# ScalarE's order within a slot: a sum's copy ahead of the scan's exponentials, in a one-core decoder layer

## What is computed

```
x = x + mamba(layernorm(x))            # dA = exp(dt*A); h = dA*h + dt*B*x; y = sum_n h*C; + D*x; 16 states
x = x + cross_attention(layernorm(x), ctx, mask)   # rmsnorm, 32 heads of 128, keys and values from ctx
x = x + ffn(layernorm(x))              # x @ W.T + b plus 16 low-rank experts
```

## Time and profile before

| | |
|---|---|
| median of three runs | 987.28 us (984.28 to 987.94) |
| the profiled execution | 985.46 us, span 983.5 us, granted TensorE clock 0.977 |
| TensorE busy | 938.3 us, 95% of the span |
| VectorE busy | 621.3 us, 63% |
| ScalarE busy | 517.1 us, 53% |
| GpSimd busy | 504.4 us, 51% |
| stage with sums and scan | to about 432 us |

### The profile page before, as it was taken

The page is one execution under the profiler, slowest core; times in us unless marked ns, Lnnn a source line. Parts: engine busy times, 40 slices in busy tenths (PEclk is TensorE's granted clock), DMA queues, the critical chain, the costliest instruction groups (busy, mean ns, idle before and its releaser), DMA issues.

```text
span 983.5 us, 14592 instructions
## 1 busy us (share of the span) xinstructions
PE 938.3 (95%) x4648; PEld 768.2 (78%) x4648; DVE 621.3 (63%) x711; ACT 517.1 (53%) x1174; POOL 504.4 (51%) x266
## 2 busy tenths in 40 slices
PE   8989989899989887999999999999999999999998
PEld 6667668687868765877888888888888888888767
DVE  5599897698899999224444444444544444444675
ACT  4776747465566653344545444544554454554531
POOL 2137496985776637413444444443644444444422
PEclk9999798999999998999999999999999999999999
DMA  8543475565665543345444444447444444444302
GB/s 289 153 151 117 148 251 180 163 190 171 203 202 172 171 157 90 129 134 165 141 137 149 136 145 154 141 136 238 142 139 141 150 147 138 138 147 136 111 14 86
DMA packets 96720, 150.03 MB, mean 153 GB/s; under 512 B 10464, under 2 KB 35168, under 8 KB 96560
## 3 DMA queue, kind: packets, MB, share of 16 engines
q1 hardware_dynamic: 87888, 132.72, 41.7%
q10 hardware_dynamic: 8800, 16.91, 6.9%
HBM read 113.81 MB, written 35.78 MB: 152 GB/s over the span
## 4 chain that ended last, share of the span: by engine, by line
PE 46%; issue 18%; DVE 13%; POOL 9%; DMA 7%; ACT 6%; ACTq 0%; POOLq 0%; SPq 0%; DVEq 0%
PE acc L423 9%; PE acc L425 9%; PE acc L424 9%; DVE misc L1076 5%; POOL wo_lo L1327 4%; POOL bm L1323 4%; PE misc L424 3%; PE misc L425 3%; PE misc L423 3%; PE acc L633 3%; DMA bc<-xp_scratch 3%; PE acc L658 3%; DMA k_scratch<-kst 3%; DVE w L1083 2%; DVE misc L1071 2%
## 5 line engine op out<-in xcount | busy, mean ns | idle before, releaser
L1307 POOL TENSOR_TENSOR wq_lo<-wq_raw,wq_hi 128x512 fp32r<-128x512 f32 x64 | 84.1, 1314 | 286.3 <-ACT wq_hi L869 286.3
L1275 POOL TENSOR_TENSOR y<-y,w 128x2048 f32<-128x2048 f32 x32 | 147.6, 4613 | 73.4 <-DVE w L1083 73.0
L1076 DVE TENSOR_TENSOR_SCAN misc<-dA,misc 128x2048 f32<-128x2048 f32 x32 | 141.7, 4429 | 24.5 <-ACT dA L739 22.4
L1172 DVE TENSOR_TENSOR ot_lo<-acc,ot_hi 128x512 fp32r<-128x512 f32 x64 | 44.2, 691 | 174.9 <-ACT ot_hi L943 174.9
L936 ACT ACTIVATE prob<-prob,negm 128x128 f32<-128x128 f32 x256 | 99.8, 391 | 78.8 <-DVE negm L1156 78.8
L423 PE MATMUL acc<-wv_hi,ctx_hi 128*128 128x512 f32 x256 | 102.5, 400 | 14.8 <-ACT vst L723 14.6
L423 PE MATMUL acc<-ctx_hi,wk_hi 128*128 128x512 f32 x240 | 98.9, 412 | 15.6 <-ACT kst L717 12.1
L925 ACT ACTIVATE q_sb<-acc 128x512 f32<-128x512 f32 x64 | 38.2, 597 | 135.3 <-PE acc L425 135.3
L423 PE MATMUL acc<-z_hi,wq_hi 128*128 128x512 f32 x256 | 106.3, 415 | 0.3 <-POOL wq_lo L1307 0.2
L423 PE MATMUL misc<-wo_hi,ot_hi 128*128 128x512 f32 x256 | 106.4, 416 | 0.0
L424 PE MATMUL misc<-wo_lo,ot_hi 128*128 128x512 f32 x256 | 101.8, 398 | 0.0
(11 more groups left out here) (160 smaller groups left out, 1959.0 us busy)
## 6 DMA issues: line engine op xcount, KB each, us to landing
k_scratch<-kst SPq DMA_DIRECT2D x64, 256.0 KB, 2.5
bc<-xp_scratch ACTq DMA_DIRECT2D x32, 512.0 KB, 5.5
v_scratch<-vst SPq DMA_DIRECT2D x32, 512.0 KB, 3.4
wq_raw<-in_wq SPq DMA_DIRECT2D x64, 256.0 KB, 3.3
k_sb<-k_scratch SPq DMA_DIRECT2D x64, 256.0 KB, 2.5
v_sb<-v_scratch SPq DMA_DIRECT2D x64, 256.0 KB, 2.6
wo_raw<-in_wo SPq DMA_DIRECT2D x64, 256.0 KB, 2.8
wraw<-in_wk SPq DMA_DIRECT2D x32, 256.0 KB, 5.7
```

The costliest lines, as they stand in the source:

```text
L1076: dve.tensor_tensor_scan(h_ps, flat(dA[k % 2][:, :, :, :]), h_ps, 0.0, ALU.mult, ALU.add).then_inc(da_free, 1)
L1172: dve.tensor_tensor(ot_lo[p][:], psO, ot_hi[p][:].bitcast(F32), ALU.subtract).then_inc(ot_lo_done, 1)
L1275: pool.tensor_tensor(y_half(half), y_half(half), w[:, k % 2], ALU.add).then_inc(y_ready, 1)
L1307: pool.tensor_tensor(wq_lo[p][:], wq_raw[p][:], wq_hi[p][:].bitcast(F32), ALU.subtract).then_inc(wq_lo_done, 1)
```

## The change

In the loop over slots of the groups 1 to 7, the copy of the slot's finished sum is issued ahead of the exponentials due in that slot, with all that hangs on them (copies and loads of B, the softplus operations). The splits of weights and the dt, transpose and z operations stay ahead of both. Nothing else changes.

```diff
                     if g < NG - 1 and slot(g, j) == split_slot(2 * g + 2):
                         split_w(2 * g + 2, wk_hi)
-                    emitted = exps(emitted, due(slot(g, j)))
                     if j < KP:
                         k_copy(g, j)
                     else:
                         v_copy(g, j - KP)
+                    emitted = exps(emitted, due(slot(g, j)))
             def split_wo(g, p):
```

## The result

The changed kernel takes 1002.05 us (median of 4 runs, 999.2 to 1003.04), and the kernel before, run beside it, 985.78 us (982.14 to 987.94): a ratio of 1.0164, with a 95% interval of 1.0124 to 1.0204. It is slower by 16.3 us, where the forecast was 995.0 with +9.5 us; that sum had the right sign and most of the right places, and was too small. The time lies at the upper end of the stated range, 984 to 1002. The profiled execution took 1001.58 us (span 999.6, granted clock 0.976). Busy times stayed as they were: TensorE has 937.7 us (938.3 before), ScalarE 516.9 (517.1). Only VectorE has 4.3 us more, 625.6 against 621.3, although no instruction was added to it.

The account below looks back on a forecast made before the run. Bound: TensorE from 70 to 378 us, waiting for ScalarE's copies, mostly held by exponentials awaiting loads of B. Terms 2.2 + 3.5 + 1.0 - 2.8 + 2.1 + 1.8 + 1.7 + 0 = +9.5 on 985.46 give 995.0 us; range 984 to 1002.

Parts of the forecast that it names:

- (a): The dt slots at (1,7): step 5's copy of B comes later, so TensorE starts (1,8) later, +2.2 us.
- (b): Slots (1,9) and (1,10): six exponentials, then a softplus exponential and weight split, delay copies; two new stalls, +3.5 us.
- (c): Loads of B shifted against SyncE's weight loads: +1.0 us for slot (1,13), -2.8 us for slot (2,15).
- (e): Slot (4,2): the split follows the wait for B in one gap, +1.8 us; half clock behind it, +1.7 us.
- (d): Slot (3,9): copies times D, an exponential and a split between two copies make slot (3,12) later, +2.1 us.
- (f): Scans and long stall at slot (6,8): VectorE 2.7 us later, but TensorE stops one sum further on; net 0.
- (g): End of the scans: TensorE's need for the last sum of y keeps enough slack, 2.7 of 7.5 us go; 0.
- renaming only: Rival: same alternation, asymmetric pieces still fit under the two sums; 985.5 us, or up to 990; chance 0.26.
- faster case: Rival: copy of (6,8) set free from six exponentials, if the scan chain starts no later; 979.1 us, chance 0.08.
- More stalls: Rival: each lengthened gap also drops the clock and loads take the long times; 1001 or 1003 us, chance 0.10.

Follow-up runs that it names:

- lag alone: Kernel before with its order kept (exponentials, then copy), but each slot gives the exponentials that were due in the slot before: 993.28 us, 1.0071.

## Why the prediction was right in sign and too small

(a), (b) and both parts of (c) held, within 0.6 us each, (b) with 4.05 us a little beyond its own bound of +3.7. The first two are where they were forecast. In (b) one row was misread: at 106.99 the fourth dt operation starts (L853), and the six exponentials run from 108.15, 5.4 us and not 6.5. After, they took 6.3 us (115.68 to 122.00), as the load of B among them, given at 115.37, was waited for 2.03 us instead of 1.13. That the size held is in part luck.

(c) was incomplete, and this is the first step that failed: it went through the loads of B against the weight loads and left out SyncE's one load of x, the largest of all. The load of B for step 9 was 1.0 us ahead of it, which the lag of one slot had to turn into 1.7 behind. With the split of (2,2) behind the wait, as in (e), the stall became 5.39 us; since the stall of 3.34 us that stood there before went at the same time, only +1.67 net is left. That older stall was not seen for what it was either: the prediction says that only the 10.82 us have a cause other than B, and this one was the store.

(d) had the right size by luck, with another cause: TensorE waits 1.52 us for GpSimd's wv_lo at 217.85, then 0.65 us in (3,12), and not 2.1 us for the copies times D. GpSimd starts this wv_lo at 213.12 instead of 201.36, 11.8 us later where the slots are some 6 later; it had worked without a pause since 181.14 (since 169.49 before). The same wv_lo holds SyncE's weight loads back to 217.90, so the load of step 15, given at 213.84, is ahead of them and not 1.5 us behind, as the term had it.

(e) measured +2.50 of +3.5. The stall grew to 2.63 us and not to 3.3, as the load of B took 4.88 us (issued at 246.55, copy at 251.43) and not the 5.55 of before (235.46, 241.01). The half clock came behind it as forecast, in this execution. The busy time of PE by stretch behind this stall, with the granted clock as third number from the end:

```profile
254.40:256.00 1.60, 1.60 (x5) 1.27 (x6) 1.50 (x2) 1.60 (x3) 1.60 (x1) 0.64 0.41 154
256.00:258.00 2.00, 2.00 (x6) 1.57 (x5) 0.91 (x1) 0.04 (x1) 2.00 (x1) 0.50 0.39 143
258.00:260.00 2.00, 2.00 (x10) 1.62 (x9) 0.00 (x0) 0.90 (x2) 2.00 (x2) 0.94 0.00 0
```

That is 0.36 of 1.6 us, half of 2.0 and 0.06 of 2.0, together 1.7 us lost, for 1.7 put down. It does not come each time: in the kernel with the split of block 13 moved, whose order is the same up to there, the clock stays at 1.00 behind a stall of 2.66 us at 252.15, and with step 5 behind the dt operations behind one of 2.53 us. That this term came out is in part luck.

(f) is the step that failed most, +5.4 us where it said net 0, and 5.1 of them are the two bold lines of the table that are marked (f). Its first half held: the scan of step 20 comes the one slot later, +3.08 for 2.7, and TensorE goes one sum further, -2.72. What failed is "everything on VectorE behind it is 2.7 us later": it took VectorE's work from there on as a fixed length. The scan of step 21, due to be free, has a wait of 0.97 us for its exponential (before, that exponential ended at 276.66, 0.12 us ahead of the scan, so there was no slack there either), and the normalisations, when shifted against GpSimd's splits, cost 4.2 us more. The four took 6.15 to 6.25 us in every kernel with the new order in group 6 but the one with the split moved, and 1.92 with the new order in group 1 only. The lag alone pays on VectorE at both steps (2.6 us, by an order of its own, and 4.4), and moving the split takes the second away. The signs given beforehand say the same: the long stall was to stay between 8 and 12 us and is 12.75, and the last scan was to end 10 to 13 us later and is 19.0 later. The trace of before had the sign: L1004 there is 4.43 us long beside y (335.39 to 339.82, y from 335.23), and wv_lo follows L1008 within 0.6 us. What (f) said of the split of (6,2) held: the stall in (6,4) grew from 2.63 to 4.09 us, and the long stall, which the scans end, took that up.

(g) held: no wait for y in the changed kernel.

Of the rivals, renaming only is out: the alternation was the same, but what stands in it ahead of and behind a wait for B was not. The faster case fell by its own condition, as the scan chain did start later. More stalls came near in the number (1001) and not in the cause: the granted clock is 1.00 behind both stalls of (b), at 122.6 and 127.3, for which that case had 1.7 us each. In the changed kernel it was 0.50 behind the stalls of 4.09, 4.14, 5.39 and 12.75 us, fell to 0.50 behind that of 2.63, and stayed at 1.00 behind those of 1.51 to 2.08; behind 2.66 and 2.53 us it stayed at 1.00 in the two kernels named under (e). By the rule of the Trainium skill's TensorE: Matmul & The Clock Gate (loop structure matters more than you think) that was weighed under renaming only, a copy out of PSUM does not break TensorE's warmth. Here what counts is that TensorE stands idle until a late copy: the order changed how long, and no run of the new order bears out "changes nothing".

One sentence of the prediction turned out better than its use: "so in plain slots a stall moves by one slot and costs what it cost". The lag by itself costs TensorE nothing in sum up to (4,4) (244.73 against 245.07). The cost is in the slots in which other work stands behind the wait instead of under it.

Open is how much of the load of step 9 is chance. Given 1.7 us behind the load of x in each, it took 10.35 us in the changed kernel, 9.54 in the one with the split of block 13 moved, whose order is the same up to there, and 9.2 with step 5 behind the dt operations. So a microsecond here, like the 1.7 us of the half clock at (4,4), can differ between two executions, and each is read from one trace.

## What to carry to other kernels

In an in-order queue, put work that waits for nothing between the issue of a load and the wait for it, never behind that wait; moving one line of a loop can undo this at each piece that stays in place. Before counting a gain of a few microseconds between two traces, look whether it lies in the stretch that the edit touches. A chain on an engine that is "never idle" is not of fixed length: look for operations in it that are long for their size, see what other engine runs beside them, and ask what a shift between the two engines makes them meet. When a stall is a wait for a chain, take time out of the chain; moving the wait gave 5 us here, and two lines that shortened the chain gave 8.

## What the runs showed of the hardware

Some of VectorE's operations stood still here while GpSimd worked. Over 128x8 a TENSOR_SCALAR took 0.17 us alone and 4.40 to 4.47 beside GpSimd, ending as GpSimd's ended (354.61 and 354.58 in the changed kernel). Four of 128x512 took 1.92 us alone and 6.02 to 6.25 beside it. In the kernel with the lag alone it hits L1007 too, a TENSOR_TENSOR of 128x8, with 4.53 us instead of 0.17. The scan (4.43 us) and the product with C (2.28 us, at 337.96 beside wv_lo from 337.74) were not slowed. The Trainium skill, SBUF — State Buffer (SBUF: two separate sides), says that VectorE and GpSimd share one pair of ports, an exclusive lock which one holds for a whole instruction while the other is fully blocked; on VectorE's side it names as taking part operations in a two-port mode and, against a GpSimd operation that reads SBUF, those with two inputs in SBUF. The trace agrees: L1007 has two inputs in SBUF (rstd, tmp) and was held, and the scan and the product with C, which have one of theirs in PSUM (misc), were not. In which mode the TENSOR_SCALAR ran, no run here shows.

A load of 512 KB, B and C of one state broadcast, took 9.2 to 10.35 us until its first reader, given 1.7 us behind a 2 MB load on another queue; 6.82 given 1.0 us ahead of it; 7.45 behind four weight loads; the median to its landing is 5.5.
